# Probabilities divided by their sums before they are transposed; their product with x Wv by seven block products for two tiles at a time

## What is computed

```python
q = x @ Wq + bq
k = x @ Wk + bk
v = x @ Wv + bv
adj = zeros((N, N)).at[edge_index[0], edge_index[1]].set(1.0)
a = q @ k.T / sqrt(q.shape[-1])
a = a * adj + (1.0 - adj) * NEG
attn = softmax(a, axis=-1)
return attn @ v
```

## Time and profile before

| what | value |
|---|---|
| median of three runs | 548.55 us (548.49 to 548.6) |
| profiled execution | 549.56 us |
| its span | 547.8 us |
| TensorE busy | 536.3 us, 98% |
| VectorE busy | 374.3 us, 68% |
| ScalarE busy | 161.6 us, 30% |
| GpSimd busy | 141.6 us, 26% |
| granted TensorE clock, mean | 0.999 |

### The profile page before, as it was taken

One profiled execution on the slowest core, in us unless ns is written; L12 is line 12 of the kernel. 1 busy time (PEld: TensorE's weight loads), 2 busy tenths in 40 slices (PEclk: granted clock), 3 DMA queues, 4 the chain that ended last, 5 costly groups with the idle time before them and its releaser, 6 DMA issues.

```text
span 547.8 us, 6788 instructions
## 1 busy us (share of the span) xinstructions
PE 536.3 (98%) x2221; PEld 355.6 (65%) x2221; DVE 374.3 (68%) x825; ACT 161.6 (30%) x349; POOL 141.6 (26%) x135
## 2 busy tenths in 40 slices
PE   8999999999999999999899999999999999999995
PEld 6555565357888888888674864544454688888643
DVE  6888888789878989356667965937384706691165
ACT  5999896471021022220120000412033100120200
POOL 3000000085228404032134900840600480000021
PEclk9999999999999999999999999999999999999999
DMA  8724000100111002000000000000050000000012
GB/s 292 266 78 151 4 1 1 41 0 1 40 40 77 1 19 78 0 1 0 2 1 0 2 0 0 1 0 1 0 211 1 0 1 0 0 1 0 1 58 98
DMA packets 12762, 20.17 MB, mean 37 GB/s; under 512 B 3243, under 2 KB 3507, under 8 KB 12726
## 3 DMA queue, kind: packets, MB, share of 16 engines
q1 hardware_dynamic: 12726, 19.69, 10.4%
HBM read 17.57 MB, written 2.11 MB: 36 GB/s over the span
## 4 chain that ended last, share of the span: by engine, by line
PE 85%; DVE 7%; ACT 3%; issue 3%; POOL 1%; DVEq 0%; POOLq 0%
PE bank L924 13%; PE bank L928 13%; PE bank L743 13%; PE bank L761 11%; PE bank L966 10%; PE bank L817 4%; PE bank L631 3%; PE bank L670 3%; PE bank L635 3%; PE bank L616 3%; PE bank L639 3%; PE bank L956 1%; DVE wk_rows L1433 1%; PE bank L647 1%; ACT apart L1041 1%
## 5 line engine op out<-in xcount | busy, mean ns | idle before, releaser
L522 POOL TENSOR_TENSOR rstd<-veps,mhalf 128x1 f32<-128x1 f32 x32 | 22.8, 712 | 197.1 <-DVE veps L1364 194.3
L966 PE MATMUL bank<-vv,probt 128*128 128x512 f32 x128 | 56.1, 592 | 0.0
L761 PE MATMUL bank<-adj,y_hi 128*128 128x512 f32 x128 | 51.3, 401 | 0.0
L1284 DVE TENSOR_TENSOR count<-bank,count 128x160 f32 x128 | 41.4, 323 | 14.0 <-PE bank L670 7.2
L761 PE MATMUL bank<-adj,y_lo 128*128 128x512 f32 x128 | 50.4, 394 | 0.0
L1371 DVE SCALAR_TENSOR_TENSOR xs<-bank,dinv,xs 128x512 f32<-128x512 f32 x23 | 17.0, 748 | 43.9 <-PE bank L817 30.5
L1041 ACT ACTIVATE apart<-col_lo,edge_key 128x128 bf16<-128x128 int16 x128 | 44.1, 396 | 1.1 <-PE bank L659 1.1
L966 PEld LDWEIGHTS bank<-vv,probt 128*128 128x128 f32 x128 | 23.9, 190 | 27.7 <-issue 27.7
L1268 DVE TENSOR_TENSOR hot_key<-col_key,key 128x320 bf16<-128x320 int16 x128 | 35.4, 316 | 0.2
L631 PE MATMUL bank<-w_sb,x0t 128*128 128x512 f32 x64 | 33.1, 601 | 0.6 <-ACT x0t L1022 0.3
L559 POOL TENSOR_SCALAR mask<-count 128x1024 bf16<-128x1024 uint16 x8 | 23.2, 2895 | 39.3 <-DVE peak L1583 29.7
(11 more groups left out here) (248 smaller groups left out, 1157.3 us busy)
## 6 DMA issues: line engine op xcount, KB each, us to landing
w_sb<-in_L_gnn_W_dram SPq DMA_DIRECT2D x3, 1024.0 KB, 6.1
xs<-in_x_dram SPq DMA_DIRECT2D x2, 1024.0 KB, 7.1
v_sb<-in_L_gnn_W_dram SPq DMA_DIRECT2D x2, 1024.0 KB, 8.1
out_dram<-xs SPq DMA_DIRECT2D x7, 256.0 KB, 2.0
w_sb<-in_L_gnn_weight_dram SPq DMA_DIRECT2D x4, 256.0 KB, 6.1
wq_sb<-in_L_gnn_Wq_dram SPq DMA_DIRECT2D x1, 1024.0 KB, 10.6
wk_sb<-in_L_gnn_Wk_dram SPq DMA_DIRECT2D x1, 1024.0 KB, 12.8
wq_rows<-in_L_gnn_Wq_dram SPq DMA_DIRECT2D x1, 1024.0 KB, 7.9
```

What stands on the lines that cost most here:

```text
L761: mm = pe.matmul(to, y[part][:, k, f * P:(f + 1) * P], m[:, k, half], start=n == 0 and part == 0 and m is mat, stop=n == NB - 1 and part = ...
L966: mm = pe.matmul(bank[:, 6 + m % 2, :], probt[:, m % 2, j, :], vv[:, j, :], start=j == 0, stop=j == NB - 1)
L1284: return V.tensor_tensor(count[:, :, bass.ds(at_dst, WIN)], bank[:, slot, n * KEYS:(n + 1) * KEYS].rearrange("p (h d) -> p h d", h=NB), co ...
```

## The change

The score products, the masks and the inputs stay as they are. Four things are new.

First, the division. `exponents` now sets `exp_set`, VectorE takes `reciprocal(m)`, and ScalarE multiplies the tile by it (`quotients(m)`), which sets `probs_set`. So the transposed blocks are probabilities.

Second, the product. For pair p (tiles p and p + 4) it is done by seven products of half size, each with 4 matmuls of 256 columns. Their operands are blocks of the transposed probabilities (`prob_low` and `prob_high`, each for one pair in turn) and of `vv`, or sums of them: four sums of `vv` made once (`sum_vv`), and four sums of probabilities for each pair (`sum_probs`, 128x512). Each product fills half of bank 6 or 7. ScalarE copies M1 out into `half_sum` (`first_mix`), VectorE adds the products to `xs` and to `half_sum` (`add_m14`, `add_m26`, `add_m57`, `add_m3`), nine additions a pair, counted by `mixed_out`.

Third, the orders. Both tiles of a pair get their moments after M3 (`pair_moments`) and are normalised together (`pair_normed`). `EAGER` is gone: ScalarE's eight `high3` all stand behind the last `first_mix`, and VectorE's `low3` three by three between the last additions.

Fourth, places. Some bias rows share the memory of `prob_high`, and the transfers of `dinv_row`, `biasc2` and `v2_sb` are issued after the last product; `v1_sb` is issued when the scores are done, as before.

```diff
+            def quotients(m):
+                act.wait_ge(exp_set, m + 1)
+                act.wait_ge(rsum_set, m + 1)
+                t = TILES[m]
+                nc.scalar.activation(score[:, m % 4, :], score[:, m % 4, :], ACT.Copy,
+                                     scale=esum[:, 1, t:t + 1]).then_inc(probs_set, 1)
+            def first_mix(p):
+                act.wait_ge(mixed, mix_at(p, "M4"))
+                if p:
+                    act.wait_ge(mixed_out, MIX_OUT * p - 1)
+                nc.scalar.copy(half_sum[:], mix_bank("M1")).then_inc(half_set, 1)
...
-                for j in range(NB):
-                    mm = pe.matmul(bank[:, 6 + m % 2, :], probt[:, m % 2, j, :], vv[:, j, :],
-                                   start=j == 0, stop=j == NB - 1)
+                left, right = {"M1": (probs[:, 0, low_keys], vv[:, low_keys, low_cols]),
+                               "M2": (probs[:, 0, high_keys], vv[:, high_keys, low_cols]),
+                               "M3": (s4, vv[:, high_keys, high_cols]), "M4": (probs[:, 1, high_keys], t4),
+                               "M5": (s1, t1), "M6": (s2, t2), "M7": (s3, t3)}[m]
+                if m == "M1":
+                    pe.wait_ge(probt_set, 2 * p + 1)
+                elif m == "M4":
+                    pe.wait_ge(probt_set, 2 * p + 2)
+                    pe.wait_ge(vv_summed, 4)
+                elif m in ("M6", "M7", "M3"):
+                    pe.wait_ge(prob_summed, 4 * p + {"M6": 2, "M7": 3, "M3": 4}[m])
+                if m == "M5":
+                    pe.wait_ge(half_set, p + 1)
+                if m in ("M5", "M3"):
+                    pe.wait_ge(mixed_out, MIX_OUT * p + {"M5": 2, "M3": 4}[m])
+                elif p and m in ("M1", "M2"):
+                    pe.wait_ge(mixed_out, taken + {"M1": 7, "M2": 9}[m])
+                for k in range(HALF):
+                    mm = pe.matmul(mix_bank(m), left[:, k, :], right[:, k, :],
+                                   start=k == 0, stop=k == HALF - 1)
...
+            mixes(2, ("M1", "M4"))
+            turn_probs(6)
+            mixes(2, ("M2", "M6"))
+            turn_probs(7)
+            mixes(2, ("M5", "M7", "M3"))
+            mixes(3, MIXES)
...
+            def add_m57(p):
+                dve.wait_ge(mixed, mix_at(p, "M7"))
+                own_mixed(p, 5)
+                to = xs[:, p:p + HALF + 1:HALF, high_cols]
+                V.tensor_tensor(to, twice(mix_bank("M5")), to, ALU.add).then_inc(mixed_out, 1)
+                V.tensor_tensor(half_sum[:], mix_bank("M7"), half_sum[:], ALU.add).then_inc(mixed_out, 1)
+                own_mixed(p, 7)
+                to = xs[:, HALF + p, :].rearrange("p (h c) -> p h c", h=2)
+                V.tensor_tensor(to, twice(half_sum[:]), to, ALU.add).then_inc(mixed_out, 1)
...
+            add_m26(3)
+            for m in range(3):
                 low3(m)
+            add_m57(3)
+            add_m3(3)
+            pair_moments(3)
+            for m in range(3, 6):
                 low3(m)
+            pair_normed(3)
```

## The result

The changed kernel takes 546.12 us (median of 15 runs, 544.99 to 548.49) against 548.87 us for the kernel before in the same 15 rounds. The ratio is 0.995, with a 95% interval of 0.9938 to 0.9963: 2.75 us less. Forecast were 546.2 us and a gain of 2.3.

A forecast was written before the change was run, and what follows sets the result against it. TensorE was taken to bound the stage, busy for all 85.57 us. 6.66 us saved less 4.35 of new waits gave 2.3 us less, 546.2 us against the median of 548.55; range 545.0 to 549.2.

The forecast's parts named there:

- The saving: On TensorE, seven half-size products a pair take 48.3 us in all against 54.96 for `mix`: gain 6.66 us.
- rival (a): Only waits built into the order (tiles 0 and 6, remnant at 1): 3.2 to 3.8 us; chance 0.13.
- case (d): On TensorE, narrow products cost more than half a wide one: 564 us; chance 0.01.
- Tile 0: TensorE's transposes wait for reciprocal and quotient, with nothing ahead to hide them: 1.40 us, 1.2 to 1.6.
- Tile 1: Transposes wait for the quotient, behind `sum_vv(3)` and the m2 addition on VectorE: 0.59 us, 0.3 to 1.1.
- Tile 2: Quotient behind `first_mix(0)` on ScalarE, yet no wait of TensorE: 0 with 0.05 us to spare, up to 0.4.
- Tile 3: Transposes wait for the quotient, behind VectorE's sums, additions and mask: 0.46 us, 0 to 1.1.
- Tile 6: Quotient queued on ScalarE behind `first_mix(2)`, so TensorE's transposes wait 1.90 us, 1.7 to 2.1.
- M1 of the last pair: Product needs VectorE's M7 addition of the pair before (same bank): wait 0, 0 to 1.0 us.
- Sum: TensorE's new waits, 1.40 + 0.59 + 0.46 + 1.90 = 4.35 us, against 6.66 saved: 2.3 us less.
- Moved work: Three `sum_vv` before the stage, the tail before layer 3 and three later loads: moved at no cost.
- (c): VectorE becomes the bound, its two-input SBUF sums slowed beside GpSimd: 4.6 us more, 550.9 us; chance 0.12.

The follow-up runs named there:

- the eighth product: Product M2 made twice for each pair in the changed kernel, 32 more records a pair; 553.04 us, ratio 1.0074 to the kernel before.
- tile 0 filled: On TensorE, score product M1 of the third pair put ahead of tile 0's transposes, against the changed kernel; 545.96 us.
- the swapped order: On ScalarE, the quotient of tile 6 put ahead of the third pair's copy of M1, against the changed kernel; 544.49 us.
- tile 3's mask first: Changed kernel reordered to fill TensorE's waits, plus `mask_scores(3)` and `reciprocal(2)` put ahead of the first pair's sums; ratio 0.9909 to the kernel before.
- one line moved: Against the run with tile 3's mask first, `reciprocal(3)` moved behind the first of three score additions; 542.93 us, ratio 0.9888.
- more sums: Changed kernel with each pair's first sum of probabilities made five times in place of once; 556.32 us, ratio 1.0138.

## Why the prediction was right, point by point

The saving, the engine that sets the time and the three largest of the four waits were right. The pattern of the waits, tiles 0, 1 and 6 and no fourth, is that of rival (a), which had a chance of 0.13, and their sum of 3.82 us lies on the border between (a) and the forecast. That the median hit 546.2 to a tenth is luck: the forecast was 0.45 too small in the gain, and it started from a median of three runs (548.55) that lay 0.32 under the later one of fifteen.

- **The bound.** TensorE sets the stage's end, and its work counts in full: shown by the eighth product (6.91 us for 32 records).
- **The saving.** 6.66 was the sum; the rows of L1011 have the duration and the load of L924's (190 ns under each record), and the spacing is 1.725 us for 8 records (352.28 to 354.01 for the first product):

```profile
352.28 1.89 PE L1011 MATMUL bank<-vv,prob_low 128*128 128x256 f32 x8
...
354.01 1.89 PE L1011 MATMUL bank<-vv_sums,prob_low 128*128 128x256 f32 x8
```

  The case (d), that loads don't hide, is excluded.
- **Tile 0.** 1.40 forecast, 1.36 measured, and 0.06 more since the transposes took 0.93 in place of 0.87 from start to start after a wait (344.66 to 345.59).
- **Tile 1.** 0.59 forecast; ready at 349.02 + 1.72 = 350.74, started at 351.35, 0.61. `sum_vv(3)` took 1.22, the lower end, though GpSimd's mask ran beside it from 0.16 us after its start; the mask took 3.67 where it has 2.77 elsewhere. The choice of the row was right, since the order of starts is the same: before, L1578 started at 348.63 and the mask at 348.79.
- **Tile 2.** 0 forecast with 0.05 to spare; none measured, with 0.23 to spare (quotient done at 358.89, TensorE there at 359.17). Tiles 5 and 7 had 0.65 and 1.15 to spare.
- **Tile 3.** 0.46 forecast, 0 measured. From the end of tile 2's reciprocal until TensorE could start, 9.60 us were taken (358.84 to 368.44) and 9.19 measured (357.64 to 366.83). No single term is far off (the mask is 361.34 to 364.06, 2.72, as taken), but operations that follow each other on VectorE start up to 0.1 us before the one ahead has ended, where I mostly added them up end to end, and handing over to TensorE takes 0.05, not 0.14. The other 0.15 is TensorE, which comes later than taken, mostly by its longer restarts at tiles 0 and 1. In the end the quotient was 0.1 us early (366.83, TensorE at 366.93), and the run with tile 0 filled shows how little was missing.
- **Tile 6.** 1.90 forecast, 1.67 and 0.06 measured. The mechanism was right, which the swapped order shows. The size was 0.2 too large: ScalarE starts the quotient 0.27 us after the copy's start rather than after its 0.37, and hands over to a waiting TensorE in 0.05 us, not 0.14 (402.77 + 1.15 to 403.97). The 0.14 came from a row in which TensorE was itself busy until then.
- **M1 of the last pair.** 0 forecast with 0.27 to spare; the addition was done at 414.03, TensorE came at 414.41.
- **Sum.** 4.35 us of waits forecast; measured 1.36 + 0.61 + 1.67 and three restarts of 0.06, 3.82. 6.66 - 3.82 = 2.84 against 2.77 in the chain. The span was put at 545.5 and measured 543.8; 1.15 of that is the earlier start of the stage.
- **Moved work.** The three `sum_vv` ahead of the stage cost nothing (1.21 to 1.22 each; the score additions were back in step one product later). TensorE has no new wait at the start of layer 3 or behind: from the last product to the span's end 117.2 us before, 117.1 after. The later transfers are hidden from it; GpSimd now waits 1.7 us once for the moved bias (L610), which no chain shows.
- **Rivals.** (c) exists as a mechanism, single sums at 1.4 to 1.5 us, but in the changed kernel its place isn't on the chain. It cost time in one run where the order alone was changed (tile 0 filled) and, together with the reciprocal's place, in the run with tile 3's mask first; with one line moved the same stretched sums cost nothing. In the run with more sums stretching and plain work were not told apart.

## What to carry to other kernels

Where one engine is busy throughout, cost a change by its work on that engine, and then walk the queues for every operation that got a longer way to it: here 6.7 us were saved and 3.8 given back in three waits, none of them visible in any engine's busy share. Before giving work to an engine with idle time, ask at which links it is idle: sixteen sums cost nothing, and sixteen more cost 69% of their time. Waits made by an order can be filled by work that needs nothing new (the products of plain blocks), but every such move shifts the others' meeting points, so read the next late link in the trace each time.

## What was not expected of the hardware

A sum of 128x512 in SBUF on VectorE took 0.68 or 1.42 to 1.52 us, depending on whether it started 0.1 us ahead of or behind a mask operation of GpSimd; so an edit on TensorE's queue alone, which brought VectorE forward by 0.7 us at this place and GpSimd by 1.3, cost 0.8 us at one sum. A TensorE that waits starts its transposes 0.05 us after ScalarE's end, and the first eight then take 0.06 us longer. The granted clock stayed at 1.00 in the changed kernel's stage, through waits of up to 1.7 us. In the run with more sums, with a wait of 3.0, it was 0.999 on the mean in the profiled execution and one other, and 0.993 to 0.996 in the three others, which were 1.4 to 3.2 us longer than the fastest; what lowered it there stays open.
